# In the late slots of a two-layer attention kernel: the values product in one piece, the next unit's first scores behind it

## What is computed

```python
def layer(x, bias, mask, ...):             # layer 0; layer 1 also normalises q and k
    xn = layernorm(x, g_in)
    q = (xn @ Wq).reshape(b, n, 16, 64).transpose(0, 2, 1, 3) * scale
    k, v = xn @ Wkv                        # one head, plus the null key and value
    sim = einsum('bhid,bjd->bhij', q, k) + bias          # scores
    sim = where(causal or masked, -max, sim)
    attn = softmax(sim)
    out = einsum('bhij,bjd->bhid', attn, v)              # values
    return layernorm(out.reshape(b, n, 1024) @ Wo, g_out)

x = x + layer0(x, ...)
x = x + layer1(x, ...)
```

## Time and profile before

| | |
|---|---|
| median of three runs | 2145.07 us (2142.49 to 2146.5) |
| profiled execution, whole | 2146.16 us |
| its span, first to last instruction | 2144.4 us |
| TensorE busy | 2084.0 us, 97% of the span |
| VectorE busy | 1601.1 us, 75% |
| ScalarE busy | 1555.1 us, 73% |
| GpSimd busy | 1027.0 us, 48% |
| granted TensorE clock, mean | 0.990 |

### The profile page before, as it was taken

One profiled execution on the slowest core, in us unless ns is written; L12 is line 12 of the kernel. 1 busy time (PEld: TensorE's weight loads), 2 busy tenths in 40 slices (PEclk: granted clock), 3 DMA queues, 4 the chain that ended last, 5 costly groups with the idle time before them and its releaser, 6 DMA issues.

```text
span 2144.4 us, 72068 instructions
## 1 busy us (share of the span) xinstructions
PE 2084.0 (97%) x26363; PEld 1860.3 (87%) x26363; DVE 1601.1 (75%) x3422; ACT 1555.1 (73%) x6241; POOL 1027.0 (48%) x1510
## 2 busy tenths in 40 slices
PE   5899999999999999999999999999999999999987
PEld 4788988988988988988988988988988988988876
DVE  5877777777777777777777777777777777777765
ACT  3767777777777777777777777777777777777775
POOL 3445444445544444544544544544544544544543
PEclk8999999999999999999999999999999999999998
DMA  7212222222222212222222222222222212222211
GB/s 233 83 55 73 63 72 62 61 60 69 66 71 60 66 59 66 70 65 61 70 58 61 75 63 63 70 57 62 75 63 63 70 57 62 75 63 63 68 52 42
DMA packets 183034, 147.47 MB, mean 69 GB/s; under 512 B 121440, under 2 KB 125616, under 8 KB 182992
## 3 DMA queue, kind: packets, MB, share of 16 engines
q1 hardware_dynamic: 179008, 141.31, 22.3%
q10 hardware_dynamic: 3296, 4.46, 0.7%
q0 software_dynamic: 688, 1.14, 0.3%
HBM read 98.56 MB, written 37.77 MB: 64 GB/s over the span
## 4 chain that ended last, share of the span: by engine, by line
PE 92%; ACT 2%; SPq 2%; DVE 2%; issue 1%; POOL 1%; DMA 0%; POOLq 0%; DVEq 0%; ACTq 0%
PE psum L709 33%; PE psum L615 18%; PE psum L581 16%; PE psum L692 8%; PE psum L674 8%; PE psum L543 3%; PE psum L632 3%; PE psum L592 2%; SPq L386 1%; ACT o_hi L907 1%; ACT probs L901 1%; POOL probs L1479 0%; DMA xa<-in_x_dram 0%; DVE wo_lo L1188 0%; PE psum L623 0%
## 5 line engine op out<-in xcount | busy, mean ns | idle before, releaser
L901 ACT ACTIVATE probs<-probs,neg_max 128x129 f32<-128x129 f32 (+3 forms) x2048 | 712.3, 351 | 56.4 <-DVE neg_max L1144 56.3
L1469 POOL TENSOR_TENSOR masked_bias<-bias,pad_neg 128x516 f32<-128x516 f32 (+3 forms) x512 | 396.2, 806 | 211.8 <-DVE probs L1138 206.1
L1479 POOL TENSOR_TENSOR probs<-probs,den_inv 128x512 f32<-128x512 f32 (+3 forms) x512 | 369.4, 743 | 149.4 <-DVE den_inv L1149 149.4
L1491 POOL TENSOR_TENSOR y_out<-y_out,res 128x512 f32<-128x512 f32 x128 | 165.9, 1296 | 527.0 <-ACT y_out L865 527.0
L901 ACT ACTIVATION_READ_ACCUMULATOR probs<-probs,neg_max 128x1 f32 x2048 | 385.4, 188 | 0.0
L1154 DVE STREAM_TRANSPOSE probs_t<-probs 128x512 f32<-128x512 f32 (+3 forms) x512 | 229.9, 487 | 196.0 <-POOL probs L1479 194.9
L1138 DVE TENSOR_TENSOR probs<-psum,masked_bias 128x648 f32<-128x648 f32 x256 | 212.7, 831 | 114.3 <-PE psum L674 110.1
L709 PE MATMUL psum<-wo_hi,o_hi 128*128 128x512 f32 x1024 | 273.2, 409 | 8.2 <-ACT o_hi L907 7.5
L907 ACT ACTIVATE o_hi<-psum,null_v_col 128x512 fp32r<-128x512 f32 x256 | 162.1, 684 | 156.0 <-PE psum L692 156.0
L709 PE MATMUL psum<-wo_hi,o_lo 128*128 128x512 f32 x1024 | 262.5, 398 | 0.0
L709 PE MATMUL psum<-wo_lo,o_hi 128*128 128x512 f32 x1024 | 261.3, 397 | 0.0
(11 more groups left out here) (133 smaller groups left out, 3915.5 us busy)
## 6 DMA issues: line engine op xcount, KB each, us to landing
res<-in_x_dram SPq DMA_DIRECT2D x64, 256.0 KB, 2.7
v_rep<-v_kept SPq DMA_DIRECT2D x512, 32.0 KB, 1.8
x_of<-y_out SPq DMA_DIRECT2D x64, 256.0 KB, 2.1
res<-x_of SPq DMA_DIRECT2D x64, 256.0 KB, 2.7
out_dram<-y_out SPq DMA_DIRECT2D x64, 256.0 KB, 2.1
xa<-in_x_dram SPq DMA_DIRECT2D x63, 256.0 KB, 2.7
xa<-x_of SPq DMA_DIRECT2D x63, 256.0 KB, 2.7
q_aside<-qp SPq DMA_DIRECT2D x32, 256.0 KB, 3.1
```

The source lines that it names most:

```text
L901: x_ = nc.scalar.activation(s, s, ACT.Exp, bias=neg_max[:, b, n:n + 1], accum_out=den[:, b, n:n + 1])
L1469: m = nc.gpsimd.tensor_tensor(block(masked_bias, b), block(bias[u.layer], b), pad_neg[u.layer][:, 0:WIDTH[b]].unsqueeze(1).to_broadcast([P ...
L1479: m = nc.gpsimd.tensor_tensor(some, some, den_inv[:, b, :].unsqueeze(2).to_broadcast([P, 4, n]), ALU.mult)
```

## The change

In `late` on TensorE the four blocks of the values are issued together, and the first half of the next unit's scores behind them. Before, the scores stood between blocks 0, 1 and blocks 2, 3. The other engines' programs are as they were.

```diff
                 if u:
                     if not w:
                         wait(pe, o_lo_done[0], u.prev)
-                    values(u, range(2))
+                    values(u, range(BLOCKS))
                 if then:
                     scores(then, 0)
-                if u:
-                    values(u, range(2, BLOCKS))
```

## The result

The changed kernel takes 2161.96 us (median of four runs, 2159.76 to 2163.68), the kernel before 2145.70 in the same session: the ratio is 1.0078, 95% interval 1.0061 to 1.0096, so 16.3 us slower. Slower was forecast, with 10.2 us; the time lies at the upper end of the range of 2148 to 2162.

What follows compares the result with a forecast made beforehand. TensorE, busy for 97% of the span, was taken to bound the kernel. Loop 10.7 us and outside the loop -0.5 gave 10.2 us, which on the median of 2145.07 makes 2155.3 us; range 2148 to 2162.

Steps and rivals of the forecast that it cites:

- VectorE is late next: Ahead of "first": VectorE's row starts 0.39 or 0.40 us later, delaying o_lo's product; loss 0.31 us a round, 0.16 contained.
- Tile shapes: In each late slot with both groups, fewer tile-shape changes save 0.23 us of TensorE's time; by that alone 15 us.
- rival A: At both followers TensorE doesn't come to wait for the addition; scores 1 end at V+2.74; 27 us faster, about 2118; 6%.
- The addition 0.40 later and TensorE's wait: In late slots the addition ends at V+3.17; TensorE resumes at V+3.31, 0.16 us later ahead of "first", 0.06 ahead of "second".
- The second place's 0.06: Ahead of "second": TensorE's product with wo goes on 0.06 us later, a loss of 0.06 in each of 29 rounds.
- The loop: Both places of the loop together: 29 x (0.31 + 0.06) = 10.7 us lost.
- The ends: Outside the loop, late0 and the late slots after it: 0.4 + 0.7 - 1.6 = -0.5 us.
- late0, where 0.4 was forecast: Ahead of the loop: late0 hands its 0.40 us delay on to the loop's first scores.
- the tail itself: Six late slots after the loop: three lose 0.3, 0.1 and 0.3 us, two gain 0.8 each, one makes no difference.
- B: Hand-over from scores 0's start to VectorE's addition is 0.89 us; no difference that can be told, about 2149 us; 16%.
- C: Register and wait instructions of TensorE's queue become visible at the transposes, resuming at V+3.5; 14.5 us, about 2159; 16%.
- D: VectorE's row absorbs its delay while waiting for ScalarE, leaving 0.16 + 0.06 a round; 6.4 us, about 2151; 14%.

Runs made afterwards that it cites:

- The runs with GpSimd's wait: GpSimd in "first" starts the masked bias only after VectorE's xn: added to the changed kernel 2155.52 us (1.0046); added to the kernel before 2145.45 (0.9997).
- the short statistics alone: Changed kernel with bn_stats of the odd unit in "first" reading 64 of 512 columns, part of the statistics left out: 2157.53 us, 1.0057.

## Why the direction was right and the size wrong: VectorE's row

The step that failed is "VectorE is late next". It put VectorE's row 0.40 us late and counted nothing for GpSimd's earlier start, and so it put the loss ahead of "first" at 0.31 us a round. The row came 0.61 late, because the normalisation took 0.84 us instead of 0.64 beside GpSimd's masked bias, and the loss was 0.46 at o_lo's product and 0.49 at the step behind it.

*Tile shapes, right as a price, not as a gain at both places.* The values take 1.35 to 1.36 us to the scores behind them at both places, as read from the earlier trace rows. Where the addition was made bank by bank the follower is earlier: 0.31 us ahead of "second", where the 0.2 us wait for o_hi goes too, and 0.13 ahead of "first". There the second scores group starts at V+2.23 and not V+1.99, behind the branch, and was at 1014.36 before, V+2.39, not at the V+2.22 that the prediction took for both places. So not all of the 0.23 could come out at the first place, and rival A's V+2.74 was out of reach there.

*The addition 0.40 later and TensorE's wait, right.* The addition starts at V+2.34, TensorE goes on at V+3.31 ahead of "first" (forecast V+3.31) and V+3.28 ahead of "second" (forecast V+3.31). The second place's 0.06 was 0.03, and by the run with that place alone it costs nothing that can be measured.

*"VectorE is late next", the step that was off.* The missing 0.20 is xn, because GpSimd's masked bias starts 1.03 us earlier. I had counted the earlier o_hi and y_out as a gain in the tail and as nothing in the loop, as GpSimd was not on the chain there; what it shares with VectorE was not in the sum. The runs with GpSimd's wait show this cause (0.84 back to 0.54, 6.4 us off the total, no effect in the kernel before), and the short statistics alone show it from the other side (1.21). A smaller error went the other way: the hand-over from o_lo to its product was put at 0.10 to 0.14. It is 0.06 where TensorE waits for it (1028.52 + 0.73 = 1029.25 to 1029.31), so the row had 0.15 us of slack and not 0.07 to 0.11. 0.61 - 0.15 = 0.46 is the loss; with xn as before it would have been 0.26. So the step's 0.31 was a little too high for the mechanism that it had, and lacked the one that cost more.

*The sum.* One normalisation of the loop, between the two places in the first round, and the same one 28 rounds later show where the 15.9 us of the span lie. VectorE before, then after:

```profile
156.67 0.55 DVE L1083 TENSOR_SCALAR xn<-xa,mv_in,rstd_in 128x512 f32<-128x512 f32 x1 [0.60 <-ACT rstd_in L842]
...
1964.65 0.55 DVE L1083 TENSOR_SCALAR xn<-xa,mv_in,rstd_in 128x512 f32<-128x512 f32 x1 [0.60 <-ACT rstd_in L842]
```

```profile
159.40 0.55 DVE L1081 TENSOR_SCALAR xn<-xa,mv_in,rstd_in 128x512 f32<-128x512 f32 x1 [0.60 <-ACT rstd_in L840]
...
1981.31 0.55 DVE L1081 TENSOR_SCALAR xn<-xa,mv_in,rstd_in 128x512 f32<-128x512 f32 x1 [0.60 <-ACT rstd_in L840]
```

Ahead of the first 2.7 us are lost, in the 28 rounds between them 13.9 (1807.98 became 1821.91, 0.50 a round, so 14.4 in 29), behind the second 0.8 won. The loop was forecast at 10.7: this is 3.7 of the error. The ends were forecast at -0.5 and came to 15.9 - 14.4 = +1.5. Of the 2.7 us, 1.6 are there already when the values of late0 start (102.35 before, 103.98 after), ahead of all changed code. Much of it is a wait for k_high, which comes from a DMA; this wait varied from 5.4 to 7.6 us in the traces of this study. The other 1.1 are behind it, at late0, where 0.4 was forecast; but a later start is partly made up for there (with the values whole ahead of "second" alone late0's start at 103.76, 1.4 late, left 0.5 at the end of the first round: 172.96 against 172.49), so late0's own share is probably nearer 2, and stays open. Behind the second row lies the place at the end of the 29th round with its 0.5 of loss, so the tail itself is 0.8 + 0.5 = 1.3 faster, and -1.6 + 0.7 = -0.9 was forecast for it.

*The rivals.* A (TensorE doesn't wait) is refuted by its 0.23 and 0.48 us of idle. B wanted 0.89 from scores 0's start to the addition: it is 1023.45 - 1022.47 = 0.98. C wanted the queue's register instructions to cost TensorE a start at V+3.5; it went on at V+3.31. Its 2159 is nearer to the result than the forecast is, by another mechanism, which is luck. D said that VectorE's row absorbs the delay: its o_lo was later than the delay itself. D's sum of 6.4 is about what is left where VectorE is given slack, 2152.37 - 2146.33 = 6.0 with short statistics and GpSimd's wait.

## What to carry to other kernels

When a reordering makes the bounding engine's own stream shorter, price first the result that the next group waits for: here 0.23 us of tile shapes were saved and 0.40 us of delay was put on one addition. Ahead of "second" it paid once the waited-for result was split so that the part needed first came first; ahead of "first" it took a shorter row of VectorE as well. And when an engine off the path gets its work earlier, look at what runs beside it at the new time: an instruction's duration is not a constant of its shape.

## What the runs showed of the hardware

*VectorE's normalisation waits for GpSimd.* The same instruction (tensor_scalar, 128x512 f32, SBUF to SBUF) took 0.54 us alone and 0.64, 0.84 and 1.21 beside a GpSimd tensor_tensor. In all three cases it ended the same time behind the GpSimd instruction that was under way: 1017.92 against 1016.34 + 1.30 = 1017.64; 1027.67 against 1026.27 + 1.11 = 1027.38; 1025.37 against 1023.97 + 1.12 = 1025.09, that is 0.28, 0.29 and 0.28. It is so in the whole trace of the kernel before: of its 128 normalisations 94 start while a GpSimd tensor_tensor is under way, and 93 of these end 0.28 or 0.29 us behind its end; the other 34 take 0.55 to 0.62. So it doesn't run at a lower rate, it stands until GpSimd's instruction is about over. GpSimd's four masked biases took 3.27 us beside it with the short statistics, and 3.10 where they came behind it. Neither the additions out of PSUM (0.83) nor the row maximum (0.69) changed.

The Trainium skill, "SBUF — State Buffer", Who interferes with whom, says that a tensor_scalar from SBUF to SBUF can enter a two-port mode, in which it and GpSimd exclude each other for a whole instruction, while tensor_reduce never contends. The trace agrees, with 0.28 or 0.29 us from GpSimd's end to VectorE's in each case, and with 0.69 for the row maximum beside GpSimd. By that rule, as an estimate, the price of moving GpSimd's work beside such an instruction is up to the length of the GpSimd instruction, 1.1 us here; what was paid was 0.10, 0.30 and 0.67.

*Hand-overs.* From scores 0's start to the addition 0.98 or 0.99 us, before and after; from the end of the addition (1023.45 + 0.83) to TensorE's next matmul 0.14, as in the earlier trace rows; from the end of o_lo's first half to its product 0.06.
